# Attention scores as float32 products of 16 rows in the row quarters of the array

## The reference

```python
q = _split_heads(Q @ W_Q.T)
k = _split_heads(K @ W_K.T)
v = _split_heads(V @ W_V.T)
scores = jnp.einsum('bhqd,bhkd->bhqk', q, k) / jnp.sqrt(jnp.float32(DK))
scores = jnp.where(mask == 0, -jnp.inf, scores)
weights = jax.nn.softmax(scores, axis=-1)
weights = jnp.nan_to_num(weights, nan=0.0)
attn = jnp.einsum('bhqk,bhkd->bhqd', weights, v)
```

## Time and profile before

| | us |
|---|---|
| median of 2 runs (1250.44 to 1254.15) | 1252.3 |
| span of the profiled execution | 1261.0 |
| TensorE busy in it (88%) | 1114.1 |
| VectorE busy (66%) | 834.2 |
| ScalarE busy (51%) | 644.9 |

### The profile page before, as it was taken

One profiled execution on the slowest core, in us unless ns is written; L12 is line 12 of the kernel. 1 busy time (PEld: TensorE's weight loads), 2 busy tenths in 40 slices (PEclk: granted clock), 3 DMA queues, 4 the chain that ended last, 5 costly groups with the idle time before them and its releaser, 6 DMA issues. The chain is left out here.

```text
span 1261.0 us, 17546 instructions
## 1 busy us (share of the span) xinstructions
PE 1114.1 (88%) x5578; PEld 545.0 (43%) x5578; DVE 834.2 (66%) x2112; ACT 644.9 (51%) x1341; POOL 211.6 (17%) x273
## 2 busy tenths in 40 slices
PE   7889999999897999999859999996979999998480
PEld 4423344434452334333446666664523333335350
DVE  5877777776577898898752222225789898868622
ACT  3446666666442776767513333322437767774240
POOL 3310000000242000010211222202410010102244
PEclk9989999999998999999959999998969999999695
DMA  8963312220069334342470220103953223201154
GB/s 252 317 205 87 88 35 81 52 52 1 1 222 274 89 104 116 93 116 62 169 279 29 102 91 29 27 22 106 330 184 107 76 64 85 64 15 67 30 155 142
DMA packets 102433, 139.38 MB, mean 111 GB/s; under 512 B 10756, under 2 KB 84360, under 8 KB 100936
## 3 DMA queue, kind: packets, MB, share of 16 engines
q1 hardware_dynamic: 98264, 128.03, 33.3%
q0 software_dynamic: 4080, 10.23, 3.0%
HBM read 86.30 MB, written 52.17 MB: 110 GB/s over the span
## 5 line engine op out<-in xcount | busy, mean ns | idle before, releaser
L888 ACT ACTIVATE r<-ps 128x512 f32<-128x512 f32 x768 | 427.8, 600 | 209.4 <-PE ps L973 126.5
L377 DVE TENSOR_REDUCE m<-ps 128x1 f32<-128x512 f32 x512 | 320.7, 683 | 38.1 <-PE ps L960 38.1
L973 PE MATMUL ps<-r 99*128 99x512 bf16 x768 | 293.6, 387 | 11.5 <-ACT r L888 5.8
L960 PE MATMUL ps<-r 96*128 96x512 bf16 x720 | 282.9, 394 | 15.0 <-DVE m L377 5.0
L990 PE MATMUL ps<-r 128*32 128x512 f32 x1536 | 199.4, 606 | 5.9 <-ACT r L888 3.3
L373 DVE CUSTOM_DVE_ANT_0 r<-ps,r 128x512 bf16<-128x512 f32 x256 | 166.6, 688 | 55.2 <-PE ps L960 54.6
L973 PEld LDWEIGHTS ps<-r 99*128 99x128 bf16 x768 | 74.7, 98 | 201.6 <-ACT r L888 114.2
L960 PEld LDWEIGHTS ps<-r 96*128 96x128 bf16 x720 | 71.1, 99 | 110.1 <-DVE m L377 29.1
L864 POOL COPY r<-r 128x256 f32<-128x256 f32 x48 | 19.1, 401 | 526.6 <-PE ps L990 526.6
L977 PE MATMUL ps<-r,identb 128*128 128x512 bf16 x256 | 97.9, 382 | 0.0
L1663 DVE COPY r<-ps 128x512 f32<-128x512 f32 x46 | 31.8, 692 | 90.4 <-PE ps L1710 90.4
(11 more groups left out here) (152 smaller groups left out, 1196.8 us busy)
## 6 DMA issues: line engine op xcount, KB each, us to landing
r<-q_parts SPq DMA_DIRECT2D x48, 384.0 KB, 4.0
r<-k_parts SPq DMA_DIRECT2D x48, 384.0 KB, 5.0
k_parts<-r SPq DMA_DIRECT2D x24, 384.0 KB, 3.2
q_parts<-r SPq DMA_DIRECT2D x24, 384.0 KB, 3.2
r<-in_w SPq DMA_DIRECT2D x16, 512.0 KB, 3.5
r<-in_w SPq DMA_DIRECT2D x8, 1024.0 KB, 14.2
k_parts<-r SPq DMA_DIRECT2D x24, 256.0 KB, 3.2
q_parts<-r SPq DMA_DIRECT2D x24, 256.0 KB, 3.1
```

What stands on the lines that cost most here:

```text
L377: ins = dve.tensor_reduce(out, mem.ps[:, bank, :], AX.X, ALU.max)
L888: act.activation(mem.probs[:, u // HG, u % HG, :], ps[:, ST + (UNITS * g + u) % DEEP, :], ACT.Exp, scale=SCALE).then_inc(a.p_exp.sem, 1)
L960: pe.matmul(ps[:, led_bank(n), :], mem.qst[g][0:ROWS, h, t * P:(t + 1) * P], mem.kst[g][0:ROWS, h, :], start=True, stop=True).then_inc(a.s ...
L973: ins = pe.matmul(out, mem.kst[g][0:KROWS, h, kt * P:(kt + 1) * P], mem.qst[g][0:KROWS, h, :], start=True, stop=not a.masked)
```

## The change

TERMS is 1 instead of 6 and PARTS 1 instead of 3. ScalarE's first part now writes the whole float32 query or key, and that is stored with one DMA; `rest`, the second part and `third` are gone. A score is one float32 product over ROWS = 16 rows, or KROWS = 17 with the row of ones and maxima. Each of the four heads of a group lies in its own 32-partition quarter of the stack (SIDES = 4, `stack_of`), so its product uses 32 rows of the array. `led_tile` orders the plain scores so that a unit's plain product lies in the quarter opposite to that of its transposed product. A stack is fetched with eight DMAs instead of two, the maxima are stored with four instead of one, and their split is one step. In xa0 the mask's product comes first and opens the bank. The stacks and the mixture's buffers move to another region, two w2 pieces are loaded after the output projection, and VectorE waits for another semaphore before it starts on the next stage's buffers.

```diff
-TERMS = 6
+TERMS = 1
 ROWS = TERMS * DK
-PARTS = 3
+PARTS = 1
 KROWS = ROWS + PARTS
+SIDES = 4
+SIDE = P // SIDES
+PAIRS = HG // SIDES
+MROWS = SIDES * PARTS * PAIRS * T
...
 def load_stacks(sp, a, b, g):
 
-    for dst, src in ((a.mem.qst[g], a.dram["q"]), (a.mem.kst[g], a.dram["k"])):
-        rows = src[b, g * GW:(g + 1) * GW, :, :].rearrange("(h r) t n -> (r t) h n", h=HG)
-        sp.dma_start(dst[0:ROWS, :, :], rows).then_inc(a.stacks[g].sem, 16)
+    for dst, src in ((a.mem.qst_in[g], a.dram["q"]), (a.mem.kst_in[g], a.dram["k"])):
+        rows = src[b, g * GW:(g + 1) * GW, :, :].rearrange("(h j r) t n -> j (r t) h n", h=PAIRS, j=SIDES)
+        for j in range(SIDES):
+            sp.dma_start(dst[j * SIDE:j * SIDE + ROWS, :, :], rows[j]).then_inc(a.stacks[g].sem, 16)
+
+
+def led_tile(v):
+
+    return (v % HG) ^ 2, v // HG
+
+
+def stack_of(stack, h, rows):
+
+    j = h % SIDES
+    return stack[j * SIDE:j * SIDE + rows, h // SIDES, :]
 
...
-    h, t = v // T, v % T
-    out = mem.m[:, t, h:h + 1]
+    h, t = led_tile(v)
+    at = h // SIDES * T + t
+    out = mem.m[:, G % 2, h % SIDES, at:at + 1]
...
-    def third(b, n):
-
-        pool.wait_ge(a.midp.sem, a.midp.at(b, n + 1))
-        pool.tensor_tensor(mem.parts[n][:, 2, :], mem.res[n % 2], mem.parts[n][:, 1, :],
-                           ALU.subtract).then_inc(a.lo.sem, 1)
-
     def body(b, ahead):
-        for n in range(QK):
-            if n == 0 and ahead is not None:
-                scale(ahead)
-            third(b, n)
+        if ahead is not None:
+            scale(ahead)
...
         act.activation(mem.parts[n][:, 0, :], ps[:, QK_BANK + n, :], ACT.Identity, bias=bias_of(a, n))\
-           .then_inc(a.hi.sem, 1)
-
-    def second_part(b, n):
-        act.wait_ge(a.r1.sem, a.r1.at(b, n + 1))
-        act.activation(mem.parts[n][:, 1, :], mem.res[n % 2], ACT.Copy).then_inc(a.midp.sem, 1)
+           .then_inc(a.r1.sem, 1)
...
-        sp.wait_ge(a.lo.sem, a.lo.at(b, n + 1))
-        runs = ((0, 3), (3, 5), (5, 6))
-        for i, (r0, r1) in enumerate(runs):
-            if of_query(n):
-                src = mem.parts[n][:, 0:r1 - r0, :]
-            else:
-                src = mem.parts[n][:, i:i + 1, :].to_broadcast([P, r1 - r0, S])
-            sp.dma_start(out[:, r0:r1, :], src).then_inc(a.stored[n].sem, 16)
+        sp.wait_ge(a.r1.sem, a.r1.at(b, n + 1))
+        sp.dma_start(out, mem.parts[n]).then_inc(a.stored[n].sem, 16)
...
-CUTS = 4
+CUTS = 1
...
         sp.wait_ge(a.m_sb.sem, a.m_sb.at(G, 1))
-        sp.dma_start(mem.qst[g][ROWS:KROWS, :, :].rearrange("a h (t n) -> a (h t) n", t=T), mem.mT[:, :])\
-          .then_inc(a.shift.sem, 16)
+        for j in range(SIDES):
+            rows = mem.qst_in[g][j * SIDE + ROWS:j * SIDE + KROWS, :, :].rearrange("a h (t n) -> a (h t) n", t=T)
+            sp.dma_start(rows, mem.mT[j * MROWS // SIDES:(j + 1) * MROWS // SIDES, :]).then_inc(a.shift.sem, 16)
...
-        h, t = v // T, v % T
+        h, t = led_tile(v)
         if used is not None:
             pe.wait_ge(a.s_max.sem, a.s_max.at(used[0], used[1] + 1))
-        pe.matmul(ps[:, led_bank(n), :], mem.qst[g][0:ROWS, h, t * P:(t + 1) * P],
-                  mem.kst[g][0:ROWS, h, :], start=True, stop=True).then_inc(a.s_ps.sem, 1)
+        pe.matmul(ps[:, led_bank(n), :], stack_of(mem.qst[g], h, ROWS)[:, t * P:(t + 1) * P],
+                  stack_of(mem.kst[g], h, ROWS), start=True, stop=True).then_inc(a.s_ps.sem, 1)
...
         out = ps[:, ST + (UNITS * g + u) % DEEP, :]
-        ins = pe.matmul(out, mem.kst[g][0:KROWS, h, kt * P:(kt + 1) * P], mem.qst[g][0:KROWS, h, :],
-                        start=True, stop=not a.masked)
         if a.masked:
-            batch = slice(b, b + 1) if type(b) is int else bass.ds(b, 1)
-            ins = pe.matmul(out, mem.identb[:, :], mem.mbT[:, batch, kt, :].rearrange("p b n -> p (b n)"),
-                            start=False, stop=True)
-        ins.then_inc(a.st_ps.sem, 1)
+            pe.matmul(out, mem.identb[:, :], mem.mbT[:, b, kt, :], start=True, stop=False)
+        pe.matmul(out, stack_of(mem.kst[g], h, KROWS)[:, kt * P:(kt + 1) * P], stack_of(mem.qst[g], h, KROWS),
+                  start=not a.masked, stop=True).then_inc(a.st_ps.sem, 1)
...
-        pe.transpose(ps[:, MISC, 0:P // 2].bitcast(BF16), mem.mparts[:, :], mem.identb[:, :]).then_inc(a.m_ps.sem, 1)
+        pe.transpose(ps[:, MISC, 0:P], mem.mparts[:, :], mem.ident[:, :]).then_inc(a.m_ps.sem, 1)
...
-        m = mem.m[:, :, :]
-        mparts = mem.mparts[:, 0:T * PARTS * HG].rearrange("p (a h t) -> p a t h", a=PARTS, h=HG)
-        hi, mid, lo = (mparts[:, i, :, :] for i in range(PARTS))
-        dve.tensor_scalar(hi, m, -1.0, None, ALU.mult).then_inc(a.cut.sem, 1)
-        dve.wait_ge(a.cut.sem, a.cut.at(G, 1))
-        dve.scalar_tensor_tensor(mem.mres[:, :, :], m, -1.0, hi, ALU.mult, ALU.subtract).then_inc(a.cut.sem, 1)
-        dve.wait_ge(a.cut.sem, a.cut.at(G, 2))
-        dve.tensor_copy(mid, mem.mres[:, :, :]).then_inc(a.cut.sem, 1)
-        dve.wait_ge(a.cut.sem, a.cut.at(G, 3))
-        dve.tensor_tensor(lo, mem.mres[:, :, :], mid, ALU.subtract).then_inc(a.cut.sem, 1)
+        m = mem.m[:, G % 2, :, :]
+        mparts = mem.mparts[:, 0:MROWS].rearrange("p (j a u) -> p a j u", j=SIDES, a=PARTS)
+        dve.tensor_scalar(mparts[:, 0, :, :], m, -1.0, None, ALU.mult).then_inc(a.cut.sem, 1)
...
-                attend_sync(sp, sa0, first_weights, lambda: last_weights(sp, me0))
+                attend_sync(sp, sa0, first_weights,
+                            lambda: last_weights(sp, me0, (sa0.pv.sem, sa0.pv.at(B * NG)), pieces[:7]))
+                last_weights(sp, me0, (sa0.op_ps.sem, sa0.op_ps.at(B)), pieces[7:])
...
-                def last_values(a):
-                    dve.wait_ge(a.vg_ready.sem, a.vg_ready.at(B * NG))
+                def last_stack(a):
+                    dve.wait_ge(a.st_ps.sem, a.st_ps.at(B * NG - 2))
```

More of the change, by code:

```diff
@@ L168, in __init__ @@
         self.cT = self.cT2[1]
[L169 to L170 removed]
+        self.parts = [take(self.r1, PARTS * S, [PARTS, S]) for _ in range(2 * C)]
         self.junk = [take(self.r1, S // 2, [S], BF16) for _ in range(8)]
```

129 lines of the change are left out of this document (60 added, 69 removed).

## The result

| | before | after |
|---|---|---|
| median (2 runs each) | 1252.3 us | 2288.5 us (2287.18 to 2289.85) |
| ratio, 95% interval | 1 | 1.827 (1.823 to 1.830) |
| span of the profiled execution | 1261.0 us | 2288.1 us |
| granted TensorE clock, mean | 0.946 | 0.632 |
| TensorE, VectorE, ScalarE busy | 88, 66, 51% | 95, 35, 28% |

What follows compares the result with a forecast made beforehand. TensorE was taken to bound the three attention stages. Profiled span 1261 + 182 (masked stage) + 144 (plain stages) - 15 (chain of parts) = 1572; the profiled execution being 8.7 above the median, 1563, given as 1560 us; range 1480 to 1870.

Steps and rivals of the forecast that it cites:

- rival 2: Attention stages: the granted clock falls; about 2270 us at half clock throughout, 1700 to 1900 for part; chance 0.14.
- the masked unit: Cross-attention of layer 0: a unit with the mask's identity product goes from 0.654 to 1.367 us, +182 us over 256.
- The 0.104 for the weights: Score products: loading 128 weight columns ahead of a first record in an empty quarter costs 0.104 us.
- the plain set: Two stages without mask: value products start at 2.90 us instead of 1.835 in four units; +144 us for both stages.
- Rival 1: Score products: quarters don't overtake, a pair's second product starts 0.43 us behind; 1820 us in all; chance 0.13.
- Rival 3: Attention stages: quarters stay full, banks and shape changes cost less, 0.27 us a product; 1320, half way 1440; chance 0.09.
- rival 4: TensorE: products of different shapes run beside each other, no change drains the array; 1235 us, not slower; chance 0.02.
- 3.07x: Skill page's speedup for four row quarters: 0.31 us a product, stages 146 us more instead of 326; not in the sum.
- the chain of parts: Projection and handovers ahead of the stages: removed splitting steps and stores save 5 us a stage, -15 us.

Runs made afterwards that it cites:

- q_full: The changed kernel with maxima in row 31, rows 16 to 30 zeroed, transposed products over 32 rows and plain over 31; 1646.3 us, 1.314 of before.
- q_rows32: The changed kernel with every score product over all 32 rows of its quarter, unused rows filled with zeros by DMAs; 1678.0 us.
- halves_full: The changed kernel turned back to bfloat16: two parts, three terms, two heads in row halves, zero-filled to 64 and 63 rows; 1219.0 us, 0.973 of before.
- before_zero_parts: The kernel before with its second and third bfloat16 parts written as zeros, all its rows kept; 1252.7 us.
- quarters_bf16: q_full with queries, keys and maxima stored as bfloat16, a single term without low parts; 1251.6 us, 0.9995 of before.

## Why the prediction was wrong

**The step that failed** is the sum's silent one: every term was priced at full clock, because the stages before had 0.98 and more, and the fall of the clock stood as rival 2 with 0.14. The argument against it was that TensorE has work in nearly every microsecond of the new stages. It had, 99%, and the clock was at the low level all the same: 0.50 in both plain stages and 0.61 in the masked one. The runs showed in its place that the clock rises with the array's rows in work: with 32 and 31 rows a product instead of 17 and 16, and nothing else that bears on TensorE, the plain stages are at 0.99 and 0.97 and the kernel at 1646 us (q_full). The one row on a low clock, the second handover at 0.69 with TensorE busy half the time, had suggested idle time as the only cause, and I took it for the rule. The 0.14 was spread over cases most of which stayed under 1870; the worst, 2270, was left out of the range.

The Trainium skill, TensorE: Matmul & The Clock Gate, Part 1, has the clock gated by how busy the engine has been, with activity releasing it. If busy means an instruction in work, the trace disagrees (504.22 of 509.30 us busy at 0.50).

**Rival 2's price** was 2270 and the time 2288, but that is luck: two errors met. The masked stage was not at the low level throughout (0.61), 683 instead of 435 + 360 = 795. The plain stages were, and took 509 instead of 280 + 175 = 455. A set of four units went from 4.46 us (q_full, 285.4/64) to 7.95 (508.9/64): 3.5 more, where 2.7 was priced. Added up by start times over the two stages, T and S take 5.2 us a set where they took 3.0 (+2.3), the value products 1.8 for 1.0 (+0.9), and turns, output projections and transposes of the maxima 0.8 for 0.5 (+0.4), which I had left out. The rows shown above give 1.8 for T and S (3.72 against 1.92) because they hold three pairs of four; the pair behind a turn costs another 0.95 (2.01 against 1.06).

**Right: the masked unit.** Forecast 1.367, measured 1.38 at full clock in the changed kernel's own trace; T and S 0.01 apart, second records 0.53 behind, the next mask product 1.06 behind the first records. The 0.104 for the weights and the changes of the array's shape, all read from other operations' rows, carried over. Stage at full clock: forecast 435, estimate from the trace 441. The stage of q_full, 487 us at 0.89, gives the same: 0.216 of it at the low level are 105 us, which at the high level would be 57, and 487 - 48 = 439.

**Right: the plain set.** Forecast about 280 us a stage, measured 285.2, 283.5 (q_rows32) and 285.4 (q_full) at 0.99, and 290.6 at 0.97. Four first records stand within 0.02 us, and the last S and the value products come 0.1 us behind their forecast times (1.94 and 3.00).

**Right: what was ruled out.** Rival 1 (no overtaking) is out by the same rows. Rival 3 (quarters full, 1320 to 1440) and rival 4 (no change of shape costs anything, 1235) are out: q_full, with a high clock, is 1646. By the 3.07x of the Trainium skill, TensorE: Matmul & The Clock Gate, Measured speedup vs the span model, the kernel would have been near 1380, an estimate from that page; q_full shows the quarters beside each other, and its rows have the waits for banks and the changes of shape that this figure leaves out.

**Mis-sized: the chain of parts.** -15 us forecast; all outside the stages was -5.5. Before the first exponential 77.6 to 77.9, between the stages 78.6 to 76.6 and 317.6 to 316.8, after the last 118.6 to 115.7. What gave back the saving of the removed parts isn't shown; the early products, in quarters now, are my guess. That there was something to be had shows in halves_full, where these stretches are 16.9 us shorter than in before_zero_parts; which part of it the low clock or the float32 bytes took in the changed kernel, I did not try.

**The sum with the clock in it.** For q_full: 1572 for the span, + 52 masked (487 for 435), + 16 plain (285.4 and 290.6 for 280 each), + 13 outside (590 for 577.5) = 1653, the profiled span of 1653.7. Of the 52 us masked 48 are the clock, as above. With filled quarters the forecast's terms come within about 5% of the kernel; without them the clock adds the rest.

## What to carry to other kernels

A product that uses few rows of the array can cost more than its streaming: before a change takes rows away from TensorE's main products, price the stage at the low clock too, and give that case a real share of the chance. Where rows stay unused, fill them with zeros to the next tile boundary: it costs TensorE nothing and, here, was worth 642 us in float32 quarters and 10 in bfloat16 halves. Start times of records carried over well from one shape to another; the clock did not. And cheaper products can lower it too: quarters_bf16 gained nothing over before.
